# A blockwise rounding split in two: the hidden tile by itself, the row tile behind the sum

## What is computed

```python
def fp4_quant_dequant(x):            # _GRID = 0, .5, 1, 1.5, 2, 3, 4, 6
    xb = x.reshape(shape[:-1] + (shape[-1] // BLOCK, BLOCK))
    scale = jnp.maximum(jnp.max(jnp.abs(xb), axis=-1, keepdims=True) / 6.0, 1e-12)
    xn = xb / scale
    idx = jnp.searchsorted(_MID, jnp.abs(xn))
    return (_GRID[idx] * jnp.sign(xn) * scale).reshape(shape)

def fp4_linear(x, w):
    return jnp.einsum('bsk,nk->bsn', fp4_quant_dequant(x), fp4_quant_dequant(w))
```

## Time and profile before

| | us |
|---|---|
| three runs | 1817.01, 1829.17, 1826.58 |
| median | 1826.58 |
| profiled execution, its own time | 1831.81 |
| its span | 1830.0 |
| TensorE busy with matmuls | 1579.2 (86%) |
| VectorE busy | 985.0 (54%) |
| ScalarE busy | 480.5 (26%) |
| GpSimd busy | 401.6 (22%) |
| first row of the changed stage's rounding (VectorE) | 1201.31 |
| first and last hidden multiplication | 1219.96, 1390.96 |

### The profile page before, as it was taken

One profiled execution on the slowest core, in us unless ns is written; L12 is line 12 of the kernel. 1 busy time (PEld: TensorE's weight loads), 2 busy tenths in 40 slices (PEclk: granted clock), 3 DMA queues, 4 the chain that ended last, 5 costly groups with the idle time before them and its releaser, 6 DMA issues. The chain is left out here.

```text
span 1830.0 us, 33671 instructions
## 1 busy us (share of the span) xinstructions
PE 1579.2 (86%) x11798; PEld 1138.1 (62%) x11830; DVE 985.0 (54%) x2514; ACT 480.5 (26%) x1041; POOL 401.6 (22%) x734
## 2 busy tenths in 40 slices
PE   4888999999968989699979899668888887999992
PEld 2664889889847744355544555445655664799891
DVE  4455334444369947766646333479877456222223
ACT  1331101011056631355622111223331431111110
POOL 0102111111042001111112244333111111344440
PEclk9998999999969998899998999878999999999996
DMA  4203989989721006234315123210000001799995
GB/s 127 51 2 125 303 296 304 298 293 307 233 61 36 2 1 173 91 92 109 86 29 170 28 80 81 67 40 18 1 1 1 2 2 47 265 320 313 314 315 176
DMA packets 162239, 240.65 MB, mean 132 GB/s; under 512 B 19824, under 2 KB 109360, under 8 KB 162000
## 3 DMA queue, kind: packets, MB, share of 16 engines
q1 hardware_dynamic: 149472, 208.35, 35.5%
q0 software_dynamic: 10512, 28.72, 5.8%
q10 hardware_dynamic: 2144, 2.10, 0.3%
HBM read 208.96 MB, written 30.15 MB: 131 GB/s over the span
## 5 line engine op out<-in xcount | busy, mean ns | idle before, releaser
L1534 DVE TENSOR_REDUCE l1a_nm<-l1a_sc 128x1 f32<-128x512 f32 (+3 forms) x256 | 107.3, 484 | 53.6 <-PE l1a_sc L1670 53.6
L2296 PEld LDWEIGHTS e0b_gp<-e0b_xT,e0b_wgu 128*128 128x128 f32 x936 | 107.4, 192 | 14.5 <-issue 12.3
L2296 PE MATMUL e0b_gp<-e0b_xT,e0b_wgu 128*128 128x128 f32 x936 | 114.9, 279 | 1.8 <-DVE e0b_hT L2366 1.3
L2317 PE MATMUL e0b_yp<-e0b_wd,e0b_hT 128*128 128x256 f32 x468 | 115.1, 388 | 0.6 <-issue 0.6
L2347 ACT ACTIVATE e0b_sg<-e0b_gp 128x640 f32<-128x640 f32 x78 | 33.5, 481 | 285.3 <-PE e0b_gp L2296 285.3
L2317 PEld LDWEIGHTS e0b_yp<-e0b_wd,e0b_hT 128*128 128x128 f32 x468 | 82.6, 189 | 21.9 <-issue 13.9
L2296 PE MATMUL e0b_up<-e0b_xT,e0b_wgu 128*128 128x128 f32 x780 | 93.5, 275 | 0.0
L2296 PEld LDWEIGHTS e0b_up<-e0b_xT,e0b_wgu 128*128 128x128 f32 x780 | 90.2, 192 | 0.0
L2296 PE MATMUL e3b_gp<-e3b_xT,e3b_wgu 128*128 128x128 f32 x624 | 77.9, 278 | 8.1 <-DMA e3b_wgu<-in_L_ffn_W 7.0
L2296 PEld LDWEIGHTS e3b_gp<-e3b_xT,e3b_wgu 128*128 128x128 f32 x624 | 73.9, 192 | 16.4 <-issue 8.3
L2451 PE MATMUL e1b_gu<-e_kgu,e1b_xT 128*128 x152 | 75.2, 617 | 4.4 <-DVE e1b_xT L2516 2.8
(11 more groups left out here) (603 smaller groups left out, 3545.7 us busy)
## 6 DMA issues: line engine op xcount, KB each, us to landing
e3b_wgu<-in_L_ffn_W SPq DMA_DIRECT2D x78, 512.0 KB
e0b_wgu<-in_L_ffn_gate_proj SPq DMA_DIRECT2D x39, 704.0 KB
e0b_wgu<-in_L_ffn_up_proj SPq DMA_DIRECT2D x39, 704.0 KB
e0b_wd<-in_L_ffn_down_proj SPq DMA_DIRECT2D x39, 640.0 KB
e3b_wd<-in_L_ffn_W SPq DMA_DIRECT2D x39, 512.0 KB
x_rows<-xn SPq DMA_DIRECT2D x3, 2048.0 KB, 8.6
l_parts<-l1p_split SPq DMA_DIRECT2D x16, 384.0 KB, 3.1
l_stack_k<-l_parts SPq DMA_DIRECT2D x48, 128.0 KB, 2.8
```

The source lines that it names most:

```text
L1534: nc.vector.tensor_reduce(nm[:, g % 2, q, i:i + 1], sc[q], AX_X, ALU.max, negate=True).then_inc(max_done, 1)
L2296: last = nc.tensor.matmul(dst[:, f, :], wgu[j][:, k, at + f * P:at + (f + 1) * P], xT[j][:, k, :], start=(k == 0), stop=(k == KC - 1))
L2317: last = nc.tensor.matmul(yp[:], hT[j][0:FW[f], f, :], wd[j][0:FW[f], f, :], start=(f == 0), stop=(f == FC - 1))
```

## The change

Tile n of VectorE's list now rounds the hidden values alone, on the semaphore `h_steps`. Statistics and sum come next. Behind them the engine waits for the normalised rows of tile n + 2 and rounds these, on `x_steps`. `invert` in tiles 1, 5 and 9 comes behind that. GpSimd's list keeps its order and only counts on the two semaphores. All operations are the same ones in the same number.

```diff
--- before.py
+++ after.py
@@ -2729,9 +2729,9 @@
                     "num", "hot", "ht", "hc", "p", "added", "recnt"))
             aggregated, rooted, inverted, shifted, xn_ready = ([sem(f"{n}{k}") for k in range(2)] for n in (
                 "agg", "root", "inv", "shift", "xn"))
-            x_steps, h_steps, both_steps, x_quant, x_turned, x_copied, tail_made, gate_made, up_made, sg_tail, sg_done, h_done, h_quant, \
+            x_steps, h_steps, x_quant, x_turned, x_copied, tail_made, gate_made, up_made, sg_tail, sg_done, h_done, h_quant, \
                 h_turned, h_copied, y_made, y_added = (sem(n) for n in (
-                    "xs", "hs", "bs", "xq", "xt", "xc", "tail", "gate", "up", "sgt", "sg", "h", "hq", "ft", "fc", "y", "ya"))
+                    "xs", "hs", "xq", "xt", "xc", "tail", "gate", "up", "sgt", "sg", "h", "hq", "ft", "fc", "y", "ya"))
             tiles = lambda b: range(b * TB, (b + 1) * TB)
             span = lambda b: slice(b * TB, (b + 1) * TB)
             gathered_in = {0: (8, 9), 1: (10, 11)}
@@ -2779,12 +2779,12 @@
                     gather(2 * TB + 2)
                     gather(2 * TB + 3)
                     for n in range(T - 2):
-                        hidden(n, both_steps, (n + 1) * 2 * QUANT_STEPS - 1)
-                        rows(n + 2, both_steps, (n + 1) * 2 * QUANT_STEPS)
+                        hidden(n, h_steps, (n + 1) * QUANT_STEPS)
+                        rows(n + 2, x_steps, (n + 3) * QUANT_STEPS)
                         if n < TB:
                             gather(3 * TB + n)
                     for n in (T - 2, T - 1):
-                        hidden(n, h_steps, (n - T + 3) * QUANT_STEPS)
+                        hidden(n, h_steps, (n + 1) * QUANT_STEPS)
 
                 @block.scalar
                 def _(act):
@@ -2987,15 +2987,14 @@
                         if n in added_in:
                             add_context(added_in[n])
                         hidden(n)
-                        if n + 2 < T:
-                            dve.wait_ge(xn_ready[1], n + 3)
-                            quantise(dve, [hidden_job(n), rows_job(n + 2)], both_steps, n * 2 * QUANT_STEPS)
-                        else:
-                            quantise(dve, [hidden_job(n)], h_steps, (n - T + 2) * QUANT_STEPS)
+                        quantise(dve, [hidden_job(n)], h_steps, n * QUANT_STEPS)
                         if n >= 3:
                             statistics(n - 3)
                         if n >= 2:
                             add(n - 2)
+                        if n + 2 < T:
+                            dve.wait_ge(xn_ready[1], n + 3)
+                            quantise(dve, [rows_job(n + 2)], x_steps, (n + 2) * QUANT_STEPS)
                         if n in added_in:
                             b = added_in[n]
                             invert(1, b)
```

## The result

The changed kernel takes 1841.93 us (median of 6 runs, 1840.44 to 1846.60), the kernel before 1821.37 us (6 runs, 1817.01 to 1829.17). The ratio is 1.0102, with a 95% interval of 1.0083 to 1.0122: slower by 15 to 22 us. The profiled execution took 1846.60 us with a span of 1844.7 us. The granted clock over the span is 0.94 in both profiles.

What follows compares the result with a forecast made beforehand. VectorE and TensorE were taken to share the bound; tile by tile, split and new hold less vanished holds and VectorE's idle time gave 19.3 us, plus 0.7: +20 on 1826.58, 1846.5 us. Own range 1840 to 1853, over the cases 1835 to 1856.

Steps and rivals of the forecast that it cites:

- the sum: Growth added over tiles 0 to 15 of the third layer's feed-forward: 19.3 us plus 0.7, so +20 us.
- The split costs 1.6 us a tile: VectorE's hidden and row rounding take 8.23 us apart against 6.64 alternating: +1.59 us in 14 tiles.
- Rival C: Splitting VectorE's rounding is free, the chain stays at 6.64 us: +2, 1829 us; chance 0.05.
- GpSimd holds the short TENSOR_SCALAR: GpSimd's hidden scaling holds the row tile's first TENSOR_SCALAR on VectorE: +0.48 us, 0.81 in tile 2, 1.14 in 0 and 1.
- Rival A: GpSimd does not hold the row tile's short TENSOR_SCALAR on VectorE: 7.8 us less, +12, 1839 us; chance 0.16.
- The holds on SCALAR_TENSOR_TENSOR go: GpSimd no longer holds these VectorE operations at tile ends: gains 1.31, 0.97, 0.64 us in tiles 0, 2, 4; 0.6 in 1.
- the 1.2 that was named as a sign: In the new profile no SCALAR_TENSOR_TENSOR pair (L2892) on VectorE should take over 1.2 us.
- VectorE becomes the bound of plain tiles: Plain tiles would follow VectorE's own work, 10.36 us each, instead of period pairs of 8.55 and 9.93 us.
- TensorE's clock falls once more: Tile 1's wait nears 5.4 us; after a 5.19 us wait the tail product took 1.65 us, not 0.92: +0.7.
- Rival B: Gate and up at half speed after the three long TensorE waits, in tiles 2, 6, 10: +7.2, 1854 us; chance 0.14.
- Rival D: TensorE's idle time covers more in tiles 6 to 14; only tiles 0 to 5 and 9 grow, 12.6 us; chance 0.05.

Runs made afterwards that it cites:

- e2: The changed kernel with the row rounding ahead of the hidden rounding, and GpSimd scaling in that order; ratio 1.0051 to the kernel before.
- e1: The changed kernel with the row rounding directly behind the hidden rounding, ahead of statistics and sum; ratio 1.0118 to the kernel before.
- e3: The kernel before with GpSimd scaling the row tile ahead of the hidden values; ratio 0.9987 to the kernel before.
- e5: The kernel before with invert directly behind the hidden multiplication in tiles 1, 5, 9 and GpSimd scaling rows first; 1813.83 us, ratio 0.9933.
- e4: The kernel before with invert and lengths directly behind the hidden multiplication in tiles 1, 5 and 9; ratio 0.9955 to the kernel before.

## Why the prediction was right

The measured difference of the medians is 20.6 us, the sum said 20. That this fits to 0.6 us is partly luck: the stage itself grew by 17.8 us, which is 2.2 under the sum, and the rest came from outside the stage. The median of 1841.93 lies 4.6 us under the forecast of 1846.5, because the kernel before had a median of 1821.37 us in that comparison instead of the 1826.58 of three runs. The tile by tile working can be set against H(n+1) - H(n) of both profiles (the windows of the earlier trace rows begin up to 0.03 us beside these starts):

| tile | expected growth | measured |
|---|---|---|
| 0 | 1.4 | 16.44 - 15.01 = 1.43 |
| 1 | 2.1 + 0.7 | 14.71 - 12.36 = 2.35 |
| 2 | 1.4 | 12.10 - 10.61 = 1.49 |
| 3 | 2.1 | 14.31 - 12.36 = 1.95 |
| 4 | 1.4 | 14.83 - 13.35 = 1.48 |
| 5 | 2.1 | 14.72 - 13.08 = 1.64 |
| 6 | 0.4 | 10.25 - 10.01 = 0.24 |
| 7 | 1.5 | 12.86 - 11.20 = 1.66 |
| 8 | 0.75 | 13.05 - 12.45 = 0.60 |
| 9 | 2.1 | 14.71 - 13.11 = 1.60 |
| 10 | 0 | 10.26 - 10.51 = -0.25 |
| 11 | 1.9 | 10.25 - 8.55 = 1.70 |
| 12 | 0.5 | 10.25 - 9.93 = 0.32 |
| 13 | 1.8 | 10.25 - 8.54 = 1.71 |
| 14 | -0.2 | 9.78 - 9.93 = -0.15 |
| sum | 20 | 17.8 |

- *The split costs 1.6 us a tile.* Right: e2, free of the hold, has plain tiles of 9.89 us against VectorE's 8.3 us before. Rival C falls. The Trainium skill, "VectorE: DVE Perf Modes", section "The DRAIN you can't avoid", found for eight copies that a semaphore after each cost nothing over one at the end. That does not carry over to these chains: 18 operations take 6.64 us in step and 8.25 us apart in e2.
- *GpSimd holds the short TENSOR_SCALAR for 0.48 us, 0.81 in tile 2, 1.14 in tiles 0 and 1.* The hold is there, and each size was 0.1 to 0.2 us too high: it is 0.36 us in ten tiles, 0.57 in tile 7, 0.69 in tile 2, and 0.96 and 1.02 in tiles 0 and 1. Each is the time to the next start less 0.09. The working let the engine go 0.03 us after GpSimd's end, at s + 1.65, as in the one row it had; in the plain tiles it went at s + 1.56. e1 gave 1.20 us without cover. Rival A falls.
- *The holds on SCALAR_TENSOR_TENSOR go.* Right for the pairs in the main: 1.24 us instead of 2.37, but not the free 1.06 that the gains were counted from, and over the 1.2 that was named as a sign. In tiles 0, 2 and 4 this 0.18 us too little and the 0.12 to 0.18 us of the hold too much cancel, so their good fit is luck. In tiles 1, 5 and 9 more was gained than counted: 0.98 us in tile 1 where I took 0.6, and I took 0 in tiles 5 and 9, yet in both the operation fell from 0.48 us in the profile before to 0.16. That and the hold make up what lies between 2.1 and 1.6. The operation now comes just ahead of GpSimd's scaling, by 0.02 us in the row shown, so this gain hangs on a near tie.
- *VectorE becomes the bound of plain tiles, at 10.36 us.* Right, at 10.25. The 0.11 us are the hold's 0.12; over some ten tiles they make up half of the 2.2 us that the sum was too high, and `invert` in tiles 1, 5 and 9 the other half.
- *TensorE's clock falls once more.* Right in place: the tail product behind the 5.52 us wait of tile 1 took 1.65 us against 0.92. Rival B did not come in tiles 6 and 10, whose clock is as before. In tile 2 the granted clock did fall, from 1.00 to 0.83, and TensorE was busy 12.10 us instead of 10.13; that hid under VectorE, since the tile grew by 1.49 us against the 1.4 of the sum, which has no such term.
- *Rival D* counted on TensorE's idle time in tiles 6 to 14. They grew by 5.8 us without tile 9, so it falls.

What the range and the chances said: 0.52 for slower by over 1% and 0.45 for within 1%; the ratio of 1.0102 lies at that bound, and its interval on both sides of it. By the stage, 17.8 us are 0.97%. So which side of 1% it is, the runs do not say.

## What to carry to other kernels

When an engine has two chains of short dependent operations, putting them in step fills the waits of each with the other; here that was worth 1.6 us in 8.2, in every tile with both jobs. Read the price of taking them apart from the places where the profile already has one chain alone. And before moving work, look at what runs beside it on the engine that can hold it: an operation of 0.17 us became one of 0.54 to 1.20 us by the company it got. The better target was elsewhere: a few small operations that release another engine stood behind 7 us of rounding. Moving them ahead, and letting GpSimd serve the job that is waited for first, made the kernel 0.7% faster.

## What was not expected of the hardware

- In these runs the hold went by who started first, within hundredths of a microsecond. In tile 5 of the changed kernel the SCALAR_TENSOR_TENSOR that started 0.02 us ahead of GpSimd was not held at all (0.16 us). In tile 5 of e3 the same operation started 0.05 us behind GpSimd (1286.42 and 1286.37) and took 1.34 us, to GpSimd's end. In e1 the TENSOR_SCALAR that started 0.22 us after GpSimd was held to its end. The second SCALAR_TENSOR_TENSOR of the changed kernel's `invert`, started while GpSimd worked, took 0.38 us.
- A pair of SCALAR_TENSOR_TENSOR that starts first gives way little to a scaling that comes between its two: 1.24 us for the pair instead of 1.06, and 0.73 us for the scaling instead of 0.62. The pair ended 0.28 us after GpSimd, and so did the pair of tile 0 in the kernel before (1229.96 and 1229.68), while its second operation takes 0.48 us when free. So some 0.2 us of it passed during the hold (an estimate from these numbers); why is open.
- TensorE still waits 3.5 us for the rows ahead of tile 6 in e5, and its granted clock there is 1.00; in e4 it waits 4.5 us and the clock is 0.85. The two edits together gained 4.2 us more in the stage than each by itself in sum. By tile it is 2.1 us in tile 6, half of it TensorE's busy time and half the wait for the rows; 0.9 in tile 5, where `invert` now stands ahead of the long scaling; 0.8 in tile 10 and 0.4 in tile 1.
